# Shift chain moved to the third burst of a step, stack loads issued ahead of it on SyncE, and the last stage's first inputs loaded in three separate steps

## The chip, the cores and the metric

The kernel runs on one core of a Trainium2 chip. The metric is device time in microseconds (us). Five engines work side by side, each through its own instruction list in order: TensorE (PE; its weight loads are shown as PEld), VectorE (DVE), ScalarE (ACT), GpSimd (POOL) and SyncE (SP), which here issues every transfer (DMA). They order one another with semaphores only, written out by hand.

## The reference, cut to what matters

```python
Q = _split_heads(x, H)                 # x: (8, 1024, 256), H = 16 heads of 16
K = _split_heads(x @ Wk + bk, H)
V = _split_heads(x @ Wv + bv, H)       # 64 columns a head
scores = einsum('bhqd,bhkd->bhqk', Q, K) + mask      # causal
attn = softmax(scores, axis=-1)
o = einsum('bhqk,bhkd->bhqd', attn, V)
x = layernorm(x + x + gelu(o) @ Wf + bf)
x = layernorm(x + (silu(x @ wg) * (x @ wu)) @ wd)    # weights: integers / 127
```

## The kernel before, in words

The work has three stages. In stage A the first two of 16 "units" (512 tokens each) are projected to keys and values. Stage B, from about 47 to 1470 us, is attention over 64 pairs of heads; beside it the projection jobs of the other 14 units are done. Stage C is the output product, both layer norms and the feed-forward part, unit by unit.

Stage B is a walk over steps `r`, each of 8 bursts `b`. PE handles pair `r` and pair `r - 2` in one step: for pair `r` it computes 12 score tiles (`score(j)`, here s0 to s11), from which DVE takes row maxima (`top(j)`), and for pair `r - 2` 12 transposed score tiles (`scoreT(t)`, here t0 to t11), which ACT exponentiates, POOL masks and adds up for the denominators, and PE multiplies with V (`weigh`). The 24 tiles go in turn through three PSUM buffers (`ring`), so a tile needs the consumer of an earlier one to be done: scoreT(3) waits for the maximum of s1, scoreT(4) for that of s2, t6 and t7 for those of s4 and s5, and t0 and t1 of the next step for s10 and s11.

A burst holds three tiles: t0, s0, t1 in burst 0; s1, t2, s2 in burst 1; t3, s3, t4 in burst 2; s4, t5, s5 in burst 3; t6, s6, t7 in burst 4, and so on.

The shift chain turns the row maxima of pair `r - 1` into two more rows of that pair's query stack, which are subtracted in the transposed scores. On DVE it is `shift_hi` (a cast of 128x16), `shift_lo` (a subtraction of 128x16) and `shift_turn` (a transpose of 128x32), each needing the one before. SP then stores the result to memory in 4 transfers (`move_shifts`, line 440), waits until they have landed and loads it in 2 (`load_shifts`, line 449). It is needed by scoreT(0) of the next step.

Projection jobs of six matmuls each lie at bursts 6, 7 and 9 counted from a step's start. By `r % 4` (called k0 to k3 here) a step starts 3, 2, 3 or 2 jobs; from step 56 on there are none. In a k0 step `x_part1`, a cast of 128x1024 on DVE, stands behind burst 2.

On SP a step is one list in order, `attend`: the shift transfers, the stacks of pair `r + 1` (`load_stacks`, 4 transfers), V (`load_v`), stores of projected tiles, of the outputs and of the denominators. In step 58 (`PAIRS - 6`) the first inputs of stage C are loaded: `load_g(0)`, `load_g(1)` (2.5 MB each with `xn`) and `load_dn(0)` (2 MB).

DVE's `shift_hi` and `shift_lo`, and POOL's masks and additions, all work from SBUF to SBUF.

Of the kernel before, what the change touches and what calls it, by code (L numbers as in the profile page):

```python
# [93 lines left out]
def build(nc, xT, x, Wk, bk, Wv, bv, Wf, bf, wg, wu, wd, out):  # L94
# [10 lines left out]
    PAIRS = B * H // 2  # L105
# [15 lines left out]
    with ExitStack() as ctx:  # L121
# [239 lines left out]
        def _(sp):  # L361
# [73 lines left out]
            def move_shifts(n):  # L435

                sp.wait_ge(s_shs, n + 1)
                settle(sp, s_passed["sp"])
                for i in range(P // SQ):
                    sp.dma_start(sd[bass.ds(n, 1)].rearrange("o h m (u s q) -> (o h m u) s q", s=P // SQ, q=SQ)[:, i],  # L440
                                  shiftT[SQ * i:SQ * (i + 1), :].bitcast(F32)).then_inc(s_shd, 16)
# [32 lines left out]
            def attend(r, it):  # L474
                n = r + RING * it
                a, k = unit_beside(r, it), r % 4
                if 1 <= r <= PAIRS:
                    move_shifts(n - 1)
                    load_shifts(r - 1, n - 1)
                if r + 1 < PAIRS:  # L480
                    load_stacks(r + 1, it)
                if k == 0 and r >= 4 and unit_beside(r - 4, it) is not None:
                    store_v(unit_beside(r - 4, it), 2)
                    store_v(unit_beside(r - 4, it), 3)
                if r < PAIRS:
                    load_v(r, it)
                if a is not None:
                    if k == 1:
                        store_k(a)
                    if k == 2:  # L490
                        store_v(a, 0)
                        if r // 4 + ALONE + 1 < UNITS:
                            load_x(a + 1)
                    if k == 3:
                        store_v(a, 1)
                if r % 4 == 3 and 7 <= r < 4 * GROUPS + 7:
                    load_den((r - 7) // 4 + it)
                if 3 <= r < PAIRS + 3:
                    store_o(r - 3, n - 3)
                    store_den(r - 3, n - 3)  # L500
                if r % 4 == 1 and 9 <= r < 4 * GROUPS + 9:
                    store_rec((r - 9) // 4 + it)
                if a is not None and k == 0:
                    store_q(a)
                if r == PAIRS - 6:

                    sp.wait_ge(s_job, NJ * UNITS)
                    sp.wait_ge(s_xs, UNITS)
                    sp.wait_ge(s_qst, 16 * 3 * UNITS)
                    sp.wait_ge(s_kst, 16 * 3 * UNITS)  # L510
                    for stored in s_vst:
                        sp.wait_ge(stored, 16 * UNITS)

                    for i in range(2):
                        sp.wait_ge(s_ost[i], 16 * (PAIRS // B // 2))
                    sp.wait_ge(s_rst, 16 * 2)
                    load_g(0, 0)
                    load_g(1, 0)
                    load_dn(0, 0)
                if r == PAIRS + LEAD:  # L520

                    sp.wait_ge(s_st, NS * PAIRS)
                    load_dn(1, 0)
# [497 lines left out]
        def _(dve):  # L1021
# [126 lines left out]
            def attend(r, it):  # L1148
                n = r + RING * it
                a, k = unit_beside(r, it), r % 4  # L1150
                for b in range(NBURST):
                    ended = job_ended(r, it, b)
                    if ended and ended[0] < DC:
                        k_part1(ended[1], ended[0], oo[0][:])
                        k_part2(ended[1], ended[0], oo[0][:])
                    if b == 0 and 1 <= r <= PAIRS:
                        shift_hi(r - 1, n - 1)
                    if b == 5 and LEAD <= r < PAIRS + LEAD:
                        carry_sum(n - LEAD)
                    for what, j in uses(b):  # L1160
                        if what == "s" and r < PAIRS:
                            top(j, r, n)
                        if what == "s" and j == 0 and 1 <= r <= PAIRS:
                            shift_lo(r - 1, n - 1)
                            shift_turn(r - 1, n - 1)
                    if b == 4 and LEAD <= r < PAIRS + LEAD:
                        begin_sum(r - LEAD, n - LEAD)
                    if a is not None and k == 0:
                        if b == 2:
                            x_part1(a)  # L1170
                        if b == 4:
                            x_part2(a)
                    if b == 7 and PAIRS <= r < PAIRS + 2:
                        norm(0, 0, range(4 * (r - PAIRS), 4 * (r - PAIRS + 1)))
                    if b == 7 and r == 0:
                        ffn_weights()
                    if b == 5 and k == 0 and 8 <= r < 4 * GROUPS + 8:
                        reciprocals((r - 8) // 4 + it, r == 8)
# [130 lines left out]
```

## Time and profile before

| what | value |
|---|---|
| median of 3 runs | 1998.43 us (1998.09 to 2004.68) |
| profiled execution, its own time | 1999.08 us |
| span of the profiled execution | 1997.3 us |
| busy: PE, DVE, POOL, ACT | 94%, 77%, 57%, 52% |
| granted TensorE clock, mean over the span | 0.97 of full speed |
| four steps of stage B with jobs, 645.0 to 731.3 us | PE 83.93 us busy of 86.3, granted clock 1.00 |
| interval between the denominator products of two steps, k0 to k1, k1 to k2, k2 to k3, k3 to k0 | 23.5, 20.6, 21.5, 20.7 us |
| the same in undisturbed steps without jobs | 20.4 to 20.5 us |
| a mask on POOL (line 632) | 0.44 us in the mean |

The page gives each engine's busy time and groups of instructions; the timeline gives instructions in order of time, with the engine's idle time before one in brackets and what ended it. PE is busy nearly all the time, so what matters is which short waits it has left, and in which step.

### The profile page before, as it was taken

Reading aid. Unit: us, or ns where it says so; the run is one execution under the profiler, and the core shown is the slowest. Engines: PE = TensorE matmul, PEld = TensorE weight load, DVE = VectorE, ACT = ScalarE, POOL = GpSimd, SP = SyncE. Lnnn points to the kernel's source line nnn. Section 1 sums busy time; section 2 is a strip of 40 time slices with the busy share of each in tenths; the row PEclk is TensorE's granted clock in tenths of the full one; section 3 lists DMA queues with packets and bytes.
Section 4 is the critical chain, followed back from the end, with each engine's and each line's share of the span. In section 5 each row is a group of like instructions: output and inputs, shape, how many; then the busy total and the mean of one; then the engine's idle time right before and its main releaser. Section 6 shows DMA issues by size and latency. Waiting matters only on the chain. (4 is left out here: it accounts for less than half of the span.)

```text
span 1997.3 us, 38522 instructions
## 1 busy us (share of the span) xinstructions
PE 1868.8 (94%) x10304; PEld 968.8 (49%) x10304; DVE 1535.2 (77%) x3597; ACT 1040.6 (52%) x1523; POOL 1139.4 (57%) x1200
## 2 busy tenths in 40 slices
PE   6799999999999999999999999878879999999996
PEld 5344444444444444444444444323337767767673
DVE  3887878888788878878788787767736887878874
ACT  2255555555655555555555555445544555655653
POOL 2177677677677677777777767766831221221212
PEclk9799999999999999999999999889989999999998
DMA  8844545554553545454464464383138666675610
GB/s 270 249 132 143 170 143 162 145 181 139 153 181 110 177 136 173 147 168 160 120 194 147 138 175 126 107 227 86 51 83 212 171 158 181 167 177 173 150 67 21
DMA packets 260962, 303.17 MB, mean 152 GB/s; under 512 B 28048, under 2 KB 177680, under 8 KB 260880
## 3 DMA queue, kind: packets, MB, share of 16 engines
q1 hardware_dynamic: 260880, 302.19, 52.5%
q8 instruction: 38, 0.62, 0.1%
q14 instruction: 44, 0.36, 0.1%
HBM read 174.20 MB, written 127.93 MB: 151 GB/s over the span
## 5 line engine op out<-in xcount | busy, mean ns | idle before, releaser
L936 ACT ACTIVATE weights<-ring 128x1024 f32<-128x1024 f32 (+3 forms) x768 | 601.3, 810 | 357.7 <-PE ring L684 355.2
L654 POOL TENSOR_TENSOR weight_sum<-weight_sum,weights 128x512 f32<-128x512 f32 (+3 forms) x448 | 682.9, 1524 | 9.7
L684 PE MATMUL o_acc<-weights,v_pair 128*64 128x512 f32 (+3 forms) x3072 | 619.4, 510 | 9.5 <-POOL weights L632 8.9
L632 POOL TENSOR_SCALAR_AFFINE_SELECT weights<-weights 128x256 f32<-128x256 f32 x512 | 224.5, 444 | 347.4 <-ACT weights L936 345.7
L1083 DVE TENSOR_REDUCE part_max<-ring 128x2 f32<-128x1024 f32 x256 | 300.2, 1214 | 104.0 <-PE ring L684 103.9
L684 PE MATMUL ring<-q_stack,k_stack 50*128 50x512 f32 (+3 forms) x1536 | 314.1, 414 | 55.2 <-DVE part_max L1083 29.3
L675 POOL TENSOR_TENSOR h_lo<-hidden,h_hi 128x512 f16<-128x512 f32 x96 | 114.5, 1194 | 399.4 <-ACT h_hi L905 399.4
L684 PE MATMUL ring<-k_stack,q_stack 48*128 48x512 f32 (+3 forms) x1536 | 307.3, 403 | 22.2 <-DMA k_stack<-k_rows 12.7
L1091 DVE CUSTOM_DVE_ANT_0 scrap<-ring,causal 128x128 bf16<-128x128 f32 (+3 forms) x512 | 229.3, 485 | 79.8 <-PE ring L684 79.3
L1091 DVE CUSTOM_DVE_ANT_0 scrap<-ring,causal,part_max 128x128 bf16<-128x128 f32 (+3 forms) x512 | 251.3, 547 | 49.6 <-PE ring L684 49.3
L684 PEld LDWEIGHTS o_acc<-weights,v_pair 128*64 128x64 f32 x3072 | 173.5, 137 | 229.9 <-issue 204.4
L684 PEld LDWEIGHTS ring<-q_stack,k_stack 50*128 50x128 f32 x1536 | 145.5, 187 | 276.1 <-DVE part_max L1083 121.6
L684 PEld LDWEIGHTS ring<-k_stack,q_stack 48*128 48x128 f32 x1536 | 147.7, 189 | 206.5 <-ACT weights L936 157.2
L684 PE MATMUL ring<-wf_sb,g 128*128 128x256 f32 x1024 | 233.0, 384 | 8.6 <-DVE y_pre L1201 8.6
L684 PEld LDWEIGHTS ring<-wf_sb,g 128*128 128x128 f32 x1024 | 195.2, 193 | 38.2 <-DVE y_pre L1201 9.0
L905 ACT ACTIVATE v_unit<-o_acc 128x512 f32<-128x512 f32 x112 | 67.0, 599 | 257.0 <-PE o_acc L684 257.0
L1146 DVE TENSOR_TENSOR g<-g,den_wide 128x512 f32<-128x512 f32 x128 | 151.0, 1204 | 1.2 <-DMA g<-o_heads 1.2
L654 POOL TENSOR_TENSOR weight_sum<-weights 128x768 f32<-128x768 f32 x64 | 116.8, 1825 | 0.0
L684 PE MATMUL o_acc<-wv_hi,x_hi 128*128 128x512 f32 x224 | 101.4, 453 | 0.0
L1125 DVE TENSOR_TENSOR weight_sum<-weights 128x1024 f32<-128x1024 f32 x64 | 78.6, 1227 | 16.4 <-PE o_acc L684 16.4
L957 ACT ACTIVATE g<-g,bv_sb 128x512 f32<-128x512 f32 x128 | 80.3, 709 | 18.3 <-DVE g L1146 18.2
L684 PE MATMUL o_acc<-wv_lo,x_hi 128*128 128x512 f32 x224 | 89.2, 398 | 0.0
(105 smaller groups left out, 2153.5 us busy)
## 6 DMA issues: line engine op xcount, KB each, us to landing
v_pairs<-v_unit SPq DMA_DIRECT2D x64, 512.0 KB, 5.6
v_pair<-v_pairs SPq DMA_DIRECT2D x64, 512.0 KB, 5.5
o_heads<-o_pair SPq DMA_DIRECT2D x64, 512.0 KB, 5.3
g<-o_heads SPq DMA_DIRECT2D x16, 2048.0 KB, 8.2
den_wide<-reciprocals SPq DMA_DIRECT2D x32, 1024.0 KB, 13.4
q_stack<-q_rows SPq DMA_DIRECT2D x128, 192.0 KB, 3.5
k_stack<-k_rows SPq DMA_DIRECT2D x128, 192.0 KB, 4.2
q_rows<-x_hi SPq DMA_DIRECT2D x32, 512.0 KB, 5.1
```

The lines of the kernel that those rows point to most:

```text
L632: pool.affine_select(out=diag, in_=diag, compare_op=ALU.is_ge, fill=0.0, base=0, pattern=[[0, 2], [1, P]], channel_multiplier=-1).then_inc ...
L654: pool.tensor_tensor(dst, other, W[t][:, :, :], ALU.add).then_inc(s_add, 1)
L675: pool.tensor_tensor(h_lo[:, f], h32[f % 2][:], h_hi[:, f], ALU.subtract).then_inc(s_hl, 1)
L684: return nc.tensor.matmul(o, l, r, start=start, stop=stop)
L905: return nc.scalar.activation(o, i, ACT.Copy)
L936: nc.scalar.activation(W[t][:, :, :], bank_of("t", t)[:, :, 0:width_of(t)], ACT.Exp).then_inc(s_w, 1)
L957: nc.scalar.activation(g[r % 2][:, c], g[r % 2][:, c], ACT.Gelu, bias=bv_sb[:, c:c + 1]).then_inc(s_gelu, 1)
L1083: v.tensor_reduce(part[r % 2][:, u - 4, :], bank_of("s", j)[:, :, 0:w], AX.X, ALU.max).then_inc(s_max, 1)
L1091: e = v.tensor_tensor_reduce(out=scrap[j % 2][h][:, 0:w], in0=bank_of("s", j)[:, h, 0:w], in1=causal[:, BANK - w:BANK], scale=1.0, scalar= ...
L1125: v.tensor_tensor(acc1[:], W[4][:], W[5][:], ALU.add).then_inc(s_add1, 1)
L1146: v.tensor_tensor(g[r % 2][:, c], g[r % 2][:, c], dn[r % 2][:, c], ALU.mult).then_inc(s_gn, 1)
```

## The change

On DVE the three parts of the shift chain no longer stand in bursts 0 and 1 but together behind burst 2. On SP the two shift steps stand behind the stack loads, the last stores of a unit's V tiles and `load_v`. The load of `g0` stays in step 58; that of the denominators goes to step 60 and that of `g1` to step 62.

```diff
             def attend(r, it):                       # SP
-                if 1 <= r <= PAIRS:
-                    move_shifts(n - 1)
-                    load_shifts(r - 1, n - 1)
                 if r + 1 < PAIRS:
                     load_stacks(r + 1, it)
...
                 if r < PAIRS:
                     load_v(r, it)
+                if 1 <= r <= PAIRS:
+                    move_shifts(n - 1)
+                    load_shifts(r - 1, n - 1)
...
                     load_g(0, 0)
+                if r == PAIRS - 4:
+                    load_dn(0, 0)
+                if r == PAIRS - 2:
                     load_g(1, 0)
-                    load_dn(0, 0)
...
                                                      # DVE
-                    if b == 0 and 1 <= r <= PAIRS:
-                        shift_hi(r - 1, n - 1)
                     if b == 5 and LEAD <= r < PAIRS + LEAD:
                         carry_sum(n - LEAD)
                     for what, j in uses(b):
                         if what == "s" and r < PAIRS:
                             top(j, r, n)
-                        if what == "s" and j == 0 and 1 <= r <= PAIRS:
-                            shift_lo(r - 1, n - 1)
-                            shift_turn(r - 1, n - 1)
...
+                    if b == 2 and 1 <= r <= PAIRS:
+                        shift_hi(r - 1, n - 1)
+                        shift_lo(r - 1, n - 1)
+                        shift_turn(r - 1, n - 1)
```

DVE, before, at the head of a step with k0, between the last row maxima of the step before and those of s4 (the two TENSOR_REDUCE of the first pair are s1 and s2, the second pair s4 and s5; a row "ISA scrap,rowmax" is one head of a maximum):

```order
L1091 ISA scrap,rowmax<-ring,causal 128x128
L1091 ISA rowmax 128x1
L1107 TENSOR_TENSOR shift_parts<-rowmax,shift_parts 128x2x8
L1116 STREAM_TRANSPOSE shiftT<-shift_parts 128x32
L1083 TENSOR_REDUCE part_max<-ring 128x2 x2
L1091 ISA scrap,rowmax<-ring,causal 128x384
L1091 ISA rowmax 128x1
L1091 ISA scrap,rowmax<-ring,causal 128x384
L1091 ISA rowmax 128x1
L1045 CAST x_hi<-xt 128x1024
L1083 TENSOR_REDUCE part_max<-ring 128x2 x2
```

The same place now; the chain has moved from ahead of s1's maximum to behind x_hi's cast, directly ahead of s4's maximum:

```order
L1085 TENSOR_REDUCE part_max<-ring 128x2 x2
L1093 ISA scrap,rowmax<-ring,causal 128x384
L1093 ISA rowmax 128x1
L1093 ISA scrap,rowmax<-ring,causal 128x384
L1093 ISA rowmax 128x1
L1047 CAST x_hi<-xt 128x1024
L1105 CAST shift_parts<-rowmax 128x2x8
L1109 TENSOR_TENSOR shift_parts<-rowmax,shift_parts 128x2x8
L1118 STREAM_TRANSPOSE shiftT<-shift_parts 128x32
L1085 TENSOR_REDUCE part_max<-ring 128x2 x2
```

SP, before, from step 58's last stores into step 59:

```order
L432 DMA o_heads<-o_pair 128x1024
L456 DMA denominators<-den_rows 4x512
L534 DMA g<-o_heads 128x8x512
L536 DMA xn<-in_x 128x4x256
L534 DMA g<-o_heads 128x8x512
L536 DMA xn<-in_x 128x4x256
L547 DMA den_wide<-reciprocals 64x8x512 x2
L440 DMA shifts<-shiftT 32x32 x4
L449 DMA q_stack<-shifts 2x1024 x2
L409 DMA q_stack<-q_rows 48x1x1024 x2
L409 DMA k_stack<-k_rows 48x1x1024 x2
L425 DMA v_pair<-v_pairs 128x8x128
```

The same place now; one of the three big loads is left, and the next step's stacks and V go ahead of the shift transfers:

```order
L432 DMA o_heads<-o_pair 128x1024
L456 DMA denominators<-den_rows 4x512
L536 DMA g<-o_heads 128x8x512
L538 DMA xn<-in_x 128x4x256
L409 DMA q_stack<-q_rows 48x1x1024 x2
L409 DMA k_stack<-k_rows 48x1x1024 x2
L425 DMA v_pair<-v_pairs 128x8x128
L440 DMA shifts<-shiftT 32x32 x4
L449 DMA q_stack<-shifts 2x1024 x2
```

## Rows read from the trace of the kernel before

**Rows 1.** Timeline of SP and PE around step 59 (start, us, engine, line, operation).
```profile
1314.80 2.61 SPq L440 DMA_DIRECT2D shifts<-shiftT  x4
...
1319.55 1.07 PE L684 MATMUL o_acc<-weight_sum,ones 128*32 128x512 f32 x8
...
1333.81 0.79 PE L684 MATMUL ring<-q_stack,k_stack 50*128 50x512 f32 x2 [4.59 <-DMA q_stack<-shifts]
...
1352.03 1.06 PE L684 MATMUL o_acc<-weight_sum,ones 128*32 128x512 f32 x8
```

**Rows 2.** Timeline of DVE, head of a k0 step to burst 3.
```profile
727.94 1.54 DVE L1103 CAST shift_parts<-rowmax 128x16 fp32r<-128x16 f32 x1
...
729.82 1.27 DVE L1107 TENSOR_TENSOR shift_parts<-rowmax,shift_parts 128x16 fp32r<-128x16 f32 x1
731.33 0.21 DVE L1116 STREAM_TRANSPOSE shiftT<-shift_parts 128x32 f32<-128x32 f32 x1 [0.24 <-DVE shift_parts L1107]
...
736.53 2.36 DVE L1083 TENSOR_REDUCE part_max<-ring 128x2 f32<-128x1024 f32 x2 [1.00 <-PE ring L684]
```

**Rows 3.** Timeline of POOL, the same stretch.
```profile
727.61 1.84 POOL L654 TENSOR_TENSOR weight_sum<-weight_sum,weights 128x768 f32<-128x768 f32 x1
...
729.77 1.28 POOL L654 TENSOR_TENSOR weight_sum<-weight_sum,weights 128x512 f32<-128x512 f32 x1
...
734.93 0.86 POOL L632 TENSOR_SCALAR_AFFINE_SELECT weights<-weights 128x256 f32<-128x256 f32 x1
735.77 2.16 POOL L654 TENSOR_TENSOR weight_sum<-weight_sum,weights 128x512 f32<-128x512 f32 x2
```

**Rows 4.** Timeline of PE, the same stretch: scoreT(4), and scoreT(7).
```profile
733.85 0.51 PE L684 MATMUL ring<-q_stack,k_stack 50*128 50x512 f32 x2 [0.45 <-DVE part_max L1083]
...
738.94 0.50 PE L684 MATMUL ring<-q_stack,k_stack 50*128 50x512 f32 x2
```

**Rows 5.** Timeline of PE and DVE in a step without jobs.
```profile
1314.85 0.33 PE L684 MATMUL ring<-q_stack,k_stack 50*128 50x128 f32 x2 [1.70 <-DVE part_max L1083]
...
1315.98 0.50 PE L684 MATMUL ring<-q_stack,k_stack 50*128 50x512 f32 x2 [0.58 <-DVE part_max L1083]
...
1318.61 2.36 DVE L1083 TENSOR_REDUCE part_max<-ring 128x2 f32<-128x1024 f32 x2 [1.74 <-PE ring L684]
```

**Rows 6.** Timeline of POOL, that step: the addition in bursts 2 and 3.
```profile
1315.37 1.82 POOL L654 TENSOR_TENSOR weight_sum<-weights 128x768 f32<-128x768 f32 x1
```

**Rows 7.** Timeline of DVE in stage C: three products back to back.
```profile
1706.82 3.37 DVE L1146 TENSOR_TENSOR g<-g,den_wide 128x512 f32<-128x512 f32 x3
```

**Rows 8.** Timeline of POOL beside them.
```profile
1707.64 1.40 POOL L675 TENSOR_TENSOR h_lo<-hidden,h_hi 128x512 f16<-128x512 f32 x1 [0.16 <-ACT h_hi L905]
```

**Rows 9.** Timeline of DVE: s4's and s5's maxima in a k1 and a k3 step.
```profile
760.03 2.36 DVE L1083 TENSOR_REDUCE part_max<-ring 128x2 f32<-128x1024 f32 x2 [1.74 <-PE ring L684]
...
802.10 2.36 DVE L1083 TENSOR_REDUCE part_max<-ring 128x2 f32<-128x1024 f32 x2 [1.24 <-PE ring L684]
```

**Rows 10.** Timeline of POOL in those two steps.
```profile
758.07 2.17 POOL L654 TENSOR_TENSOR weight_sum<-weight_sum,weights 128x512 f32<-128x512 f32 x2
759.50 0.73 POOL L654 TENSOR_TENSOR weight_sum<-weight_sum,weights 128x256 f32<-128x256 f32 x1
...
800.59 2.16 POOL L654 TENSOR_TENSOR weight_sum<-weight_sum,weights 128x512 f32<-128x512 f32 x2
```

**Rows 11.** Timeline of DVE: two small operations, the second needing the first.
```profile
1717.29 0.17 DVE L1261 SCALAR_TENSOR_TENSOR newton<-mean_var,rstd 128x8 f32<-128x8 f32 x1 [0.61 <-ACT rstd L1015]
1717.50 0.17 DVE L1264 TENSOR_TENSOR newton<-newton,rstd 128x8 f32<-128x8 f32 x1
```

**Rows 12.** Windows: busy time of each engine, granted clock, DMA share, GB/s.
```profile
1270.00:1275.00 5.00, 4.74 (x16) 1.48 (x16) 1.98 (x5) 1.90 (x3) 4.52 (x6) 0.50 0.22 56
```

**Rows 13.** DMA view: transfers, size, median us to landing.
```profile
v_pairs<-v_unit SPq DMA_DIRECT2D x64, 512.0 KB, 5.6
...
shifts<-shiftT SPq DMA_DIRECT2D x256, 4.0 KB, 1.3
```

## Prediction

> **What bounds the kernel now.** I read the page first: PE is busy for 94% of the span, and in four steps with jobs for 83.9 of 86.3 us, so there all waits that a change could take away sum to 2.4 us. Then I read the timeline of PE step by step, taking the denominator products as marks, to see which short waits are left, and the timelines of DVE and POOL beside them, to see what makes them.
>
> Three things stand out. First, one step is far too long: between the marks at 1319.55 and 1352.03 lie 32.48 us, where a step without jobs takes 20.45 [rows 1]. SP issued the shift transfers of that step behind seven MB of loads for stage C; they went out at 1314.80 and PE still waited for the shift rows at 1333.81 (4.59 us), and again 4.59 us for the next stack behind them, with the clock at its lower level afterwards.
>
> Second, the shift chain costs DVE far more than its work. The cast of 128x16 took 1.54 us and ended at 729.48, when POOL's addition ended (727.61 + 1.84 = 729.45); the subtraction took 1.27 and ended at 731.09, when POOL's next addition ended (729.77 + 1.28 = 731.05) [rows 2, 3]. Each began just after POOL's. The smallest such operations take 0.17 us. So DVE and POOL exclude one another in these operations, for the whole of an instruction. The Trainium skill says the same (SBUF — State Buffer, "Who interferes with whom": a cast in a 2-port mode or an operation with two SBUF inputs blocks or is blocked by GpSimd for a whole instruction), and the trace agrees.
>
> Third, who waits: behind the chain stand the maxima of s1 and s2, and scoreT(3) and scoreT(4) need them. In a k0 step PE waited 0.45 us at scoreT(4) [rows 4]; the k1 and k2 steps have the same row with 0.39 and 0.46, k3 none. In a step without jobs PE waited 1.70 + 0.58 us [rows 5].
>
> **The big loads.** In the new order step 58 ends with 2.5 MB, step 60 with 2 MB, step 62 with 2.5 MB. The old seven MB went out from 1301.9 on and the shift rows behind them were there only at 1333.8 [rows 1], some 30 us, so a third of them takes about 10 us; it is issued some 15 us into a step of 20 and is over before the next step's shift transfers, which are also later now. I take the whole excess as gone: 32.48 - 20.45 = **-12.0 us**. If one part is still felt, this is less (a rival below).
>
> **The chain's old place.** Without it the maxima of s1 and s2 come as early as PE allows. With jobs, scoreT(4) comes 0.45 (k0), 0.39 (k1), 0.46 (k2) and 0 us (k3) earlier. Without jobs s1 is ready at 1312.3, its maximum takes half of 2.36, s2's the other half, so scoreT(4) can start at about 1314.71 and not 1315.98 [rows 5]: 1.27 us earlier.
>
> **The chain's new place.** It stands ahead of s4's maximum, where DVE idled for 1.00 to 1.74 us [rows 2, 5, 9]. But this gap is not free time. The two maxima of s4 and s5 end at 736.53 + 2.36 = 738.89, and scoreT(7), which needs s5's, starts at 738.94 [rows 4]; in each kind of step I found these 0.05 us. Every microsecond by which s4's maximum starts later than 0.54 us behind the start of its matmul is one that PE waits at scoreT(6) and (7). So I have to place the chain against POOL. Three prices: the cast ends 0.03 us behind the POOL operation it waits for; the subtraction asks 0.04 later (a dependent small operation started at 1717.50 behind one that ended at 1717.46 [rows 11]); the transpose comes 0.24 later and takes 0.21 [rows 2]. And a rule: three DVE products back to back took 3.37 us from 1706.82, and POOL's operation from 1707.64 to 1709.04 ran between the first two [rows 7, 8]. So whoever already waits goes next, and the engine that has just finished does not keep the right.
>
> - k0: x_hi's cast ends at 736.53 - 1.00 = 735.53. POOL's mask (734.93, 0.86 long, so itself held up) goes next and ends at 735.79, the chain's cast at 735.82, and the addition from 735.77, which was already waiting, holds the subtraction until 735.77 + 1.28 = 737.05 [rows 3]. The transpose ends at 737.53; s4's maximum starts at 737.47 instead of 736.53: **+0.94 us**.
> - k1: DVE is free at 760.03 - 1.74 = 758.29, POOL's addition has just begun at 758.07 and ends at 759.35, the second one starts only at 759.50 because it depends on the first [rows 9, 10]. The cast ends at 759.38, the subtraction asks at 759.42, 0.08 us ahead of the second addition, and gets in; the transpose ends at 760.04: s4's maximum starts at 759.98, **-0.05**.
> - k2: the cast waits for the end of an addition at 779.2, the subtraction for a mask, until 779.6; the transpose ends at 780.05, ahead of s4's maximum at 780.22. The gain stands whole: **-0.46**.
> - k3: DVE is free at 802.10 - 1.24 = 800.86, POOL's addition began at 800.59 and ends at 801.87. As in k1 the subtraction gets in ahead of the second one; the transpose ends at 802.57, s4's maximum starts at 802.52: **+0.42**.
> - without jobs: DVE is free at about 1315.62, the addition of 1.82 us that began at 1315.37 holds the cast until 1317.2 [rows 6], a mask the subtraction until 1317.6, and s4's maximum starts at 1317.93 where it started at 1318.61 [rows 5]: **-0.68**.
>
> Four steps with jobs: 0.94 - 0.05 - 0.46 + 0.42 = +0.85 us, a small loss. There are 13 such groups (steps 4 to 55): **+11.1 us**. Seven steps without jobs (57 to 63): 7 x -0.68 = **-4.8 us**. The steps ahead of 4 and behind 63 have nothing on POOL beside the chain: 0.
>
> **The clock.** In stage B without jobs the granted clock fell to 0.50, the lower of the two levels (1.2 GHz), for some microseconds in three steps, each time behind PE's waits at scoreT(3) and (4) [rows 12]; these steps took 23.07, 21.91 and 22.03 us instead of 20.45, together 5.7 us more. The waits there shrink from 2.28 to about 1.0 us, with 0.6 put in at scoreT(6). Four steps with the full waits did not lose the clock, so this is no switch; between 0 and 5.7 I take half: **-2.8 us**.
>
> **SP.** The shift transfers now go out about 6 us later in a step. The stack loads need the previous step's last scoreT and go out at once; load_v and the V stores stand ahead of the shift transfers. In k0 the last V store waits for ACT's copy of the last job (about 5.6 us into the step), load_v for that store's landing (5.6 us [rows 13]), so the shift transfers go out some 12 us into the step, queue behind 512 KB (5.6 at most), then the loads: about 19 us, in a step of 23.5. In the other steps they land about 15 us into 20.6. The stores behind them (keys, V, outputs) come up to 6 us later, and their readers stand in later steps. Cost 0, hidden by the rest of the step, 4.5 us in the tightest case.
>
> **The sum.** -12.0 + 11.1 - 4.8 - 2.8 = -8.5 us against the execution's own 1999.08, which lies 0.65 above the median: 1990.6; against the median 1989.9. I say **1990 us**. The step's own range is 1982 to 1998.
>
> **Rivals.**
> 1. *The second addition wins.* In k1 and k3 the subtraction beats POOL's second addition by 0.08 us only. Losing it costs 0.73 less the 0.1 us or so of overlap: +0.6 in each, +1.2 in a group, 13 groups: +15.6, time 2006. For it: the margin is smaller than what I know of each price, and the skill's page cited above says only that whoever starts first holds the port. Against it: POOL's pause between the two is in both steps. 15%.
> 2. *The chain is hidden.* DVE gets in sooner than I placed it, in k0 above all, or the loss there is swallowed by a later wait. At the far end nothing is lost at s4: 13 x -1.3 = -17, 7 x -1.27 = -9, -12 and the whole clock term -5.7: 1955. Getting only k0 free (-1.4 a group, -18) gives 1972. For it: the idle time is there; against it: the ends of POOL's and DVE's operations coincide within 0.04 us. 17%, most of it near 1972.
> 3. *Slower: the shift rows come too late.* In k0 steps the chain of store, load_v, shift store and shift load has 4.5 us of room by my count. If each landing takes 2.5 us longer than in the median, scoreT(0) of the k1 step waits; with 3 us in 13 steps this is +39, about 2029. It decides from some 5 us later than computed. For it: the landings are medians and 1.3 us [rows 13] was taken where nothing else was in flight. The Trainium skill gives a DMA a fixed cost of about 2 us (DMA: Bandwidth & Descriptors, "Anatomy of one DMA"), longer than this row; by it two landings would come 1.4 us later, still inside the room. 11%.
> 4. *The loads are still felt.* One of the three parts delays a stack or shift rows as much as all together did: -12 becomes 0, time 2002. 7%.
>
> The forecast has 50%. Faster by over 0.5% (10 us, about what a measurement of this kernel can tell from no change) means below 1988.4: rival 2 and two fifths of the forecast, 0.37. Slower means above 2008.4: rival 3 and a little of rival 1: 0.13. The rest, 0.50, is the same. The range of 1970 to 2012 leaves out the far ends of rivals 2 and 3.
>
> **What the changed profile would show.** The step with the big load back at 20 to 22 us and no wait for shift rows or stacks. No wait at scoreT(3) in job steps, and none or less at scoreT(4). The cast at burst 3 at 0.3 to 1.6 us, ending with a POOL addition; the subtraction long (about 1.2 us) in k0 and short in k1 and k3. New waits of PE for DVE at scoreT(6) or (7), about 0.9 us in k0, 0.4 in k3. The groups of four at about 87.1 us instead of 86.3. I am wrong if these groups get shorter, if the subtraction is long in k1 and k3 too, or if PE waits for "q_stack<-shifts" at the head of steps.

## The result, and the profile after

The kernel after takes 2019.08 us in the median (2015.39 to 2020.07), the kernel before 1998.26 in the runs beside it: ratio 1.0096, 95% interval 1.0069 to 1.0124. It is slower by about 1%, where I forecast 1990. The profiled execution took 2019.51 us, 20.4 more than that of before.

The page's head, with busy time and share of each engine:

```profile
span 2017.8 us, 38472 instructions
...
PE 1863.2 (92%) x10304; PEld 967.2 (48%) x10304; DVE 1547.3 (77%) x3597; ACT 1043.9 (52%) x1523; POOL 1126.2 (56%) x1200
```

PE's share fell from 94 to 92%. DVE is busy 12 us longer than before (1535.2), although it does the same operations: more of its time is time in which it stood blocked. Windows of the kernel after, first four steps with jobs, then three without (us, busy time and count of PE, PEld, DVE, ACT, POOL, granted clock, DMA share, GB/s):

```profile
647.85:736.61 88.76, 84.07 (x478) 37.34 (x476) 71.10 (x172) 47.80 (x69) 62.42 (x68) 0.98 0.52 150
...
1308.76:1329.67 20.91, 17.11 (x107) 6.65 (x105) 17.95 (x41) 11.21 (x16) 15.42 (x18) 1.00 0.33 92
1329.67:1352.38 22.71, 18.65 (x106) 7.12 (x104) 18.23 (x42) 11.18 (x16) 16.04 (x18) 0.92 0.71 199
1352.38:1372.99 20.61, 17.11 (x106) 6.65 (x105) 17.39 (x45) 11.22 (x16) 14.91 (x18) 1.00 0.35 94
```

The group of four took 86.3 us and takes 88.76. PE's busy time in it is nearly the same (83.93 and 84.07), so PE waits 2.3 us more. The interval behind step 59's mark, which took 32.48 us [rows 1], is the window of 20.61 now: the big load's stall is gone. The window of 22.71 is the one before it, 20.45 in before; it has the longest of the new waits (below) and a granted clock of 0.92. What PE waits for stands in its timeline (denominator products of a k0, k1, k2, k3 and k0 step are the rows with `weight_sum,ones`; the first two waits are those of the k2 step, then those of k0; the last rows are from a step without jobs):

```profile
668.32 1.07 PE L686 MATMUL o_acc<-weight_sum,ones 128*32 128x512 f32 x8
...
693.83 1.07 PE L686 MATMUL o_acc<-weight_sum,ones 128*32 128x512 f32 x8
...
714.06 1.06 PE L686 MATMUL o_acc<-weight_sum,ones 128*32 128x512 f32 x8
715.91 0.50 PE L686 MATMUL ring<-q_stack,k_stack 50*128 50x512 f32 x2 [0.78 <-DVE part_max L1085]
...
717.04 0.50 PE L686 MATMUL ring<-q_stack,k_stack 50*128 50x512 f32 x2 [0.51 <-DVE part_max L1085]
...
736.61 1.06 PE L686 MATMUL o_acc<-weight_sum,ones 128*32 128x512 f32 x8
...
757.09 1.07 PE L686 MATMUL o_acc<-weight_sum,ones 128*32 128x512 f32 x8
759.81 0.50 PE L686 MATMUL ring<-q_stack,k_stack 50*128 50x512 f32 x2 [1.66 <-DVE part_max L1085]
...
760.94 0.65 PE L686 MATMUL ring<-q_stack,k_stack 50*128 50x512 f32 x2 [0.51 <-DVE part_max L1085]
...
1324.97 0.33 PE L686 MATMUL ring<-q_stack,k_stack 50*128 50x128 f32 x2 [0.59 <-DVE part_max L1085]
...
1326.10 0.50 PE L686 MATMUL ring<-q_stack,k_stack 50*128 50x512 f32 x2 [0.58 <-DVE part_max L1085]
...
1332.35 0.50 PE L686 MATMUL ring<-q_stack,k_stack 50*128 50x512 f32 x2 [1.62 <-DVE part_max L1085]
...
1333.48 0.50 PE L686 MATMUL ring<-q_stack,k_stack 50*128 50x512 f32 x2 [0.51 <-DVE part_max L1085]
```

The marks stand behind scoreT(4) and ahead of scoreT(6). The intervals between them are 25.51 (k0 to k1), 20.23, 22.55 and 20.48 us; in before they were 23.5, 20.6, 21.5 and 20.7. The wait at scoreT(4) [rows 4] is gone in these steps, and waits at scoreT(6) and scoreT(7) have come: 2.17 us in k0, 1.29 in k2.

Part of the loss in k0 is clock. In the 13 groups of before the granted clock was 1.00 from end to end. In the kernel after it fell to 0.50, the lower of the two levels, for some microseconds in 12 of the 13 intervals k0 to k1, each time right behind these two waits of PE. The first window is an interval that kept the clock, the second one that lost it, the third lies inside the second:

```profile
225.75:250.58 24.83, 21.70 (x125) 9.77 (x123) 21.93 (x52) 11.52 (x17) 17.03 (x18) 1.00 0.55 161
668.32:693.83 25.51, 22.96 (x125) 10.30 (x123) 21.88 (x52) 11.59 (x17) 16.48 (x18) 0.93 0.51 156
673.00:675.00 2.00, 2.00 (x8) 0.48 (x6) 2.00 (x2) 1.02 (x1) 0.00 (x0) 0.50 0.03 8
```

Eleven such intervals took 25.39 to 25.65 us, and the first, where the lower level stayed longer, 26.92. Against the 24.83 of the one without it that is some 9 us in the 13 groups. The k2 steps, with waits of 0.78 and 0.51 us, kept the clock.

DVE at the same places shows the reason for the waits:

```profile
711.81 2.25 DVE L1105 CAST shift_parts<-rowmax 128x16 fp32r<-128x16 f32 x1
714.10 0.18 DVE L1109 TENSOR_TENSOR shift_parts<-rowmax,shift_parts 128x16 fp32r<-128x16 f32 x1
714.52 0.21 DVE L1118 STREAM_TRANSPOSE shiftT<-shift_parts 128x32 f32<-128x32 f32 x1 [0.25 <-DVE shift_parts L1109]
714.65 2.33 DVE L1085 TENSOR_REDUCE part_max<-ring 128x2 f32<-128x1024 f32 x2
...
754.62 2.73 DVE L1047 CAST x_hi<-xt 128x1024 fp32r<-128x1024 f32 x1
757.27 0.70 DVE L1105 CAST shift_parts<-rowmax 128x16 fp32r<-128x16 f32 x1
758.01 0.17 DVE L1109 TENSOR_TENSOR shift_parts<-rowmax,shift_parts 128x16 fp32r<-128x16 f32 x1
...
758.56 2.33 DVE L1085 TENSOR_REDUCE part_max<-ring 128x2 f32<-128x1024 f32 x2
...
1326.91 3.68 DVE L1105 CAST shift_parts<-rowmax 128x16 fp32r<-128x16 f32 x1
```

And POOL beside them:

```profile
710.57 1.85 POOL L656 TENSOR_TENSOR weight_sum<-weights 128x768 f32<-128x768 f32 x1
712.34 0.44 POOL L634 TENSOR_SCALAR_AFFINE_SELECT weights<-weights 128x256 f32<-128x256 f32 x1
712.72 2.19 POOL L656 TENSOR_TENSOR weight_sum<-weight_sum,weights 128x512 f32<-128x512 f32 x2
...
753.35 1.84 POOL L656 TENSOR_TENSOR weight_sum<-weights 128x768 f32<-128x768 f32 x1
755.12 0.44 POOL L634 TENSOR_SCALAR_AFFINE_SELECT weights<-weights 128x256 f32<-128x256 f32 x1
755.49 2.45 POOL L656 TENSOR_TENSOR weight_sum<-weight_sum,weights 128x512 f32<-128x512 f32 x2
...
1327.11 1.84 POOL L656 TENSOR_TENSOR weight_sum<-weights 128x768 f32<-128x768 f32 x1
1328.89 0.42 POOL L634 TENSOR_SCALAR_AFFINE_SELECT weights<-weights 128x256 f32<-128x256 f32 x1
1329.27 2.17 POOL L656 TENSOR_TENSOR weight_sum<-weight_sum,weights 128x512 f32<-128x512 f32 x2
```

In the k2 step the cast stood ready at 711.81, while the addition of 710.57 ran. It did not get in when that ended (712.42), nor when the mask behind it ended (712.78). It ended at 714.06, at the end of the next addition, where POOL has its one pause (the two additions of the row of 712.72 depend on each other and lie 0.15 us apart). In the k0 step x_hi's cast, 0.87 us long before, waited in the same way and took 2.73. In the step without jobs the shift cast took 3.68 us for work of 0.17. That is the longest of the seven such steps; two of the others got in at the first end (0.24 and 0.23 us).

The whole difference, by marks of the two traces, where the loads and the chain are still mixed: up to the mark of step 4 +1.8 us, the 13 groups (steps 5 to 56) +32.6, steps 57 to 63 -15.3, steps 64 to 66 +1.7, the rest -0.4.

### The profile page after: what moved, and what is told of

The parts are those of the page before. It is cut to its first block and busy times, and to the rows that moved or that the text cites. A ratio compares the mean times of both kernels' runs of the same rounds, so it can differ in the third digit from the quotient of the medians.

```text
span 2017.8 us, 38472 instructions
## 1 busy us (share of the span) xinstructions
PE 1863.2 (92%) x10304; PEld 967.2 (48%) x10304; DVE 1547.3 (77%) x3597; ACT 1043.9 (52%) x1523; POOL 1126.2 (56%) x1200
## 5 line engine op out<-in xcount | busy, mean ns | idle before, releaser
L686 PE MATMUL o_acc<-weights,v_pair 128*64 128x512 f32 (+3 forms) x3072 | 629.3, 517 | 14.9 <-POOL weights L634 10.1
L634 POOL TENSOR_SCALAR_AFFINE_SELECT weights<-weights 128x256 f32<-128x256 f32 x512 | 211.1, 418 | 392.0 <-ACT weights L938 378.4
L686 PE MATMUL ring<-q_stack,k_stack 50*128 50x512 f32 (+3 forms) x1536 | 308.7, 405 | 79.3 <-DVE part_max L1085 68.6
L686 PE MATMUL ring<-k_stack,q_stack 48*128 48x512 f32 (+3 forms) x1536 | 302.1, 396 | 18.3 <-DMA k_stack<-k_rows 9.0
```

The source lines that it names most:

```text
L634: pool.affine_select(out=diag, in_=diag, compare_op=ALU.is_ge, fill=0.0, base=0, pattern=[[0, 2], [1, P]], channel_multiplier=-1).then_inc ...
L686: return nc.tensor.matmul(o, l, r, start=start, stop=stop)
```

## The experiments

The kernels of the experiments were timed in five rounds each; a ratio is to the kernel before on the same chip. For each, the length of two stretches of its profiled execution: the 13 groups with jobs, and steps 57 to 63.

| kernel | median us | ratio, 95% interval | 13 groups | 57 to 63 |
|---|---|---|---|---|
| before | 1998.3 | | 1119.6 | 160.8 |
| after | 2019.1 | 1.0069 to 1.0124 | 1152.2 | 145.5 |
| chain only | 2033.1 | 1.0150 to 1.0192 | 1150.8 | 160.0 |
| SP order only | 1999.1 | 0.9986 to 1.0014 | 1119.1 | 161.2 |
| three loads only | 1987.1 | 0.9924 to 0.9961 | 1119.3 | 148.7 |
| after, two-input first part | 2016.7 | 1.0068 to 1.0108 | 1151.3 | 144.4 |
| after, pause ahead of mask 3 | 1985.2 | 0.9909 to 0.9950 | 1122.8 | 141.2 |
| after, two short additions | 1961.0 | 0.9785 to 0.9830 | 1099.2 | 140.7 |
| after, chain behind fourth burst | 2012.1 | 1.0037 to 1.0082 | 1148.0 | 141.4 |
| three loads only, same pause | 1986.8 | 0.9919 to 0.9960 | 1119.5 | 148.7 |
| after, pause ahead of mask 2 | 1988.2 | 0.9923 to 0.9967 | 1124.2 | 142.9 |
| chain behind fourth burst, pause | 1990.9 | 0.9944 to 0.9973 | 1127.0 | 143.6 |
| pause, k0's chain behind fourth burst | 1979.4 | 0.9879 to 0.9923 | 1115.8 | 141.6 |
| pause, x_hi behind fourth burst | 1969.9 | 0.9837 to 0.9884 | 1107.1 | 142.7 |

### The three parts of the change alone

**Chain only**: the kernel before with the DVE part of the change.

```diff
-                    if b == 0 and 1 <= r <= PAIRS:
-                        shift_hi(r - 1, n - 1)
...
-                        if what == "s" and j == 0 and 1 <= r <= PAIRS:
-                            shift_lo(r - 1, n - 1)
-                            shift_turn(r - 1, n - 1)
...
+                    if b == 2 and 1 <= r <= PAIRS:
+                        shift_hi(r - 1, n - 1)
+                        shift_lo(r - 1, n - 1)
+                        shift_turn(r - 1, n - 1)
```

> The kernel before with one part of the change: the three shift operations on DVE behind burst 2; SP's order and the big loads as before. Theory P (the cast waits for POOL through several operations in a row, ahead of the maximum of s4, and PE then waits at scoreT(6) and (7)): all of the loss is here. From the changed kernel's steps: +34 us up to step 56, some -3 in the steps without jobs, +2 behind them, and the 12 us of the big load stay: about 2030 us. Rival S (the later shift transfers on SP, or the loads ahead of them, make the loss): no loss here, 1998 or a few us less, since scoreT(3) and (4) no longer wait.

**SP order only**: the two shift steps behind `load_v`.

```diff
-                if 1 <= r <= PAIRS:
-                    move_shifts(n - 1)
-                    load_shifts(r - 1, n - 1)
...
                     load_v(r, it)
+                if 1 <= r <= PAIRS:
+                    move_shifts(n - 1)
+                    load_shifts(r - 1, n - 1)
```

> The kernel before with SP's new order alone: stack loads, V stores and load_v ahead of the shift transfers, DVE and the big loads as before. Theory P: no difference but in the step with the big load, 1990 to 1999 us. Rival S: slower by 20 us or more, with waits of PE for shift rows or stacks.

**Three loads only**:

```diff
                     load_g(0, 0)
+                if r == PAIRS - 4:
+                    load_dn(0, 0)
+                if r == PAIRS - 2:
                     load_g(1, 0)
-                    load_dn(0, 0)
```

> The kernel before with the last stage's first inputs loaded in steps 58, 60 and 62 and nothing else changed. By the prediction's term the long step shrinks from 32.5 to 20.5 us and the whole by 12: 1986 us. If each part is felt alone, between 1990 and 1998.

Measured: +34.3, +0.4 and -11.7 us to the before of the same chip (1998.77). They add to +23.0, where all together gave +20.8. So the SP order is neutral, the loads gave what they should, and the whole loss is the chain's place on DVE. With the chain alone the interval with the big load's stall takes 38.2 us instead of 32.48, which is part of the 34.3.

### What kind of operation waits

The chain's first part as an operation with two SBUF inputs (the maximum of the row maxima with themselves, the same values) instead of a cast:

```diff
-                v.tensor_copy(shift_parts[:, :, 0], rowmax[r % 2][:]).then_inc(s_shp, 1)
+                v.tensor_tensor(shift_parts[:, :, 0], rowmax[r % 2][:], rowmax[r % 2][:],
+                                ALU.max).then_inc(s_shp, 1)
```

> The changed kernel with the cast of shift_hi written as a maximum of the row maxima with themselves, a TENSOR_TENSOR with two SBUF inputs that gives the same values. In both traces all 65 subtractions that met POOL got in at the end of the very next POOL operation, while the cast at burst 3 did so in 3 of about 70 cases where POOL's operations followed without a pause. Theory P, with the kind of operation deciding: the first operation now lasts at most 1.8 us (until POOL's next end), 0.3 in k2 steps where it was 2.25, up to 1.8 where it was 3.7; gain 1.5 x 13 in k2 steps and about 1 x 7 without jobs: 1990 to 1997 us. If only the place among POOL's operations decides and not the kind: 2019 as the changed kernel.

Measured: 2016.74, as the kernel after. DVE's timeline, the k2 step:

```profile
709.43 2.20 DVE L1105 TENSOR_TENSOR shift_parts<-rowmax 128x16 fp32r<-128x16 f32 x1
```

It waits 2.20 us where the cast waited 2.25. That it could pass where a cast can't is refuted: the kind of operation does not matter, only that it comes first at this place.

### A pause in POOL's run

If DVE gets in only where POOL pauses, a pause one addition earlier must let it in. POOL's fourth mask waits for the end of the addition just ahead of it, which is a wait of some 0.17 us and orders nothing new:

```diff
             def mask(t, rt, n):
                 pool.wait_ge(s_w, NS * n + t + 1)
+                if t == 3:
+                    pool.wait_ge(s_add, NA * n + 1)
                 settle(pool, s_passed["pool"])
```

> The changed kernel with one more wait on POOL: the mask of t3 waits for the first addition of the pair, which stands directly ahead of it, so that POOL pauses there some 0.15 us as it does between its second and third additions. At that pause DVE got in every time. Theory P (DVE gets in only where POOL pauses, once POOL has run for long without one): the first shift operation in k2 steps ends 0.03 us behind the first addition (0.3 us instead of 2.25) and the interval k2 to k3 falls from 22.5 to about 21; x_hi's cast in k0 steps takes 0.8 to 1 instead of 2.7 and the interval k0 to k1 falls from 25.5 to 24.4 or less. 13 x 2.6 and 7 x 1: about 1980 us. Rival K (POOL's total work in this stretch delays DVE, the pause changes nothing): 2019 to 2022.

> Control to the pause: the kernel with the three separate loads and the chain in its old place, 1987.1 us, with the same added wait on POOL. The pause by itself should cost nothing (POOL is idle 5 us a step) and may let x_hi's cast in earlier in the few steps where it was held up: 1984 to 1989. If the wait itself gives or takes time, it shows here.

Measured: 1985.18 us, 34 less than the kernel after; the same pause with the chain in its old place (beside the three loads) gives 1986.75, where the loads alone gave 1987.12. So the pause costs and gives nothing by itself, and it takes nearly the whole of the chain's +34 away. DVE in a k2 step of the kernel with the pause:

```profile
698.16 0.64 DVE L1107 CAST shift_parts<-rowmax 128x16 fp32r<-128x16 f32 x1
698.84 0.17 DVE L1111 TENSOR_TENSOR shift_parts<-rowmax,shift_parts 128x16 fp32r<-128x16 f32 x1
```

and POOL:

```profile
696.95 1.82 POOL L658 TENSOR_TENSOR weight_sum<-weights 128x768 f32<-128x768 f32 x1
698.94 0.41 POOL L636 TENSOR_SCALAR_AFFINE_SELECT weights<-weights 128x256 f32<-128x256 f32 x1 [0.17 <-POOL weight_sum L658]
```

The cast ends 0.03 us behind the addition (698.77), as my prediction had it for the kernel after. The shorter waits also cost less clock: it fell in 5 of the 13 groups instead of 12. Two k0 to k1 intervals of this kernel have the same waits (0.77 and 0.5 us) and take 24.57 us with the lower level in them and 23.86 without.

**Short additions**: POOL's second and third additions cover only the last 8 of their 512 columns, so the denominators lack the rest of these sums.

```diff
+                if t in (2, 3):
+                    pool.tensor_tensor(dst[:, :, w - 8:w], other[:, :, w - 8:w],
+                                       W[t][:, :, w - 8:w], ALU.add).then_inc(s_add, 1)
+                else:
+                    pool.tensor_tensor(dst, other, W[t][:, :, :], ALU.add).then_inc(s_add, 1)
```

> The changed kernel with most of POOL's second and third additions of each pair left out: they add the last 8 columns of each head alone, so the denominators are incomplete and only the time is read. Theory P: the first shift operation can at most wait for the first addition and a mask and then meets a pause, so the chain no longer delays s4's maximum by more than 0.5 us: 2.8 us less in a group of four steps, 1.5 in a step without jobs, 1970 to 1985. If PE's waits at scoreT(6) and (7) have another cause than POOL's additions: 2010 to 2019.

Measured: 1961.01, below what I expected. The groups take 84.6 us; the waits at scoreT(6) and (7) are gone but for 0.4 us in k0, and the clock never fell in them. It agrees with POOL's operations being all that stands in the chain's way, but it also takes work from POOL that other operations of DVE waited for, so it gives a bound and not a share.

### Is it the pause, or how long POOL has run?

The place of the cast and the length of POOL's run ahead of it were mixed up till then. This kernel pauses one place earlier, ahead of the third mask; the end of the 768-wide addition and the mask behind it are back to back again, only soon after a pause:

```diff
+                if t == 2:
+                    pool.wait_ge(s_sel, NM * n + masked(1))
```

> As the kernel after, but POOL's pause stands one place earlier: ahead of the third mask (mask 2) instead of ahead of the fourth, so the end of the first addition (128x768) and mask 3 behind it are back to back again, only that POOL has by then run three operations (about 2.7 us) since its last pause instead of 13 or more. Theory 1 (the length of POOL's unbroken run decides whether the waiting DVE operation gets in between two back-to-back POOL operations): the cast gets in at the end of the first addition, as with the pause at that place, and the time is near 1985. Theory 2 (the place decides: the boundary between that addition and the mask never lets DVE in, or only a real pause does): the casts in k2 and in the steps without jobs wait until the pause behind the second addition, as in the kernel after, and the time stays near 2017. A third result would be casts that get in at the earlier pause only in k3 and k1: 2005 to 2015. I expect theory 1 with 60%.

Measured: 1988.16. DVE, a k2 step:

```profile
698.28 0.81 DVE L1107 CAST shift_parts<-rowmax 128x16 fp32r<-128x16 f32 x1
699.12 0.32 DVE L1111 TENSOR_TENSOR shift_parts<-rowmax,shift_parts 128x16 fp32r<-128x16 f32 x1
```

POOL beside it:

```profile
696.87 0.41 POOL L636 TENSOR_SCALAR_AFFINE_SELECT weights<-weights 128x256 f32<-128x256 f32 x1 [0.16 <-POOL weights L636]
697.24 1.82 POOL L658 TENSOR_TENSOR weight_sum<-weights 128x768 f32<-128x768 f32 x1
699.01 0.41 POOL L636 TENSOR_SCALAR_AFFINE_SELECT weights<-weights 128x256 f32<-128x256 f32 x1
699.38 1.28 POOL L658 TENSOR_TENSOR weight_sum<-weight_sum,weights 128x512 f32<-128x512 f32 x1
```

The addition ends at 699.06, the cast at 699.09 and the subtraction at 699.44, at the end of the mask. At exactly this end of the addition, of the casts that stood waiting (19 shift casts and 13 of x_hi), none of 32 got in in the kernel after, and 32 of 32 do here. The first theory holds in this comparison: a real pause at the place itself is not needed, one two operations earlier is enough. In the kernel after two subtractions did get in at this end, both 0.03 us behind a cast that had itself just got in.

### Where else to put the chain

**Chain behind the fourth burst**, no pause:

```diff
-                    if b == 2 and 1 <= r <= PAIRS:
+                    if b == 3 and 1 <= r <= PAIRS:
                         shift_hi(r - 1, n - 1)
```

> The changed kernel with the shift chain one burst later, behind the maxima of s4 and s5, where POOL's third addition ends and POOL is then idle for about 6 us. Theory P: the three operations take 0.17 + 0.17 + 0.24 + 0.21 us, nothing waits at scoreT(6) and (7); s6's maximum comes some 0.4 us later, which may cost 0 to 0.3 a step at scoreT(9). Against before the waits at scoreT(4) are gone (1.3 us in four steps with jobs, 1.3 in each without) and so are the 12 us of the loads: 1955 to 1975 us. If the chain costs wherever it stands behind burst 2 (or its later transfers come too late): 1998 or more.

Measured: 2012.07, a miss. The chain itself runs free there, but the 13 groups are as long as after. DVE, a k0 step:

```profile
662.26 2.49 DVE L1047 CAST x_hi<-xt 128x1024 fp32r<-128x1024 f32 x1
...
666.93 0.16 DVE L1105 CAST shift_parts<-rowmax 128x16 fp32r<-128x16 f32 x1
```

PE, the same step:

```profile
667.07 0.50 PE L686 MATMUL ring<-q_stack,k_stack 50*128 50x512 f32 x2 [0.52 <-DVE part_max L1085]
...
672.80 0.44 PE L686 MATMUL ring<-q_stack,k_stack 50*128 50x384 f32 x2 [1.48 <-DVE rowmax L1093]
```

x_hi's cast, which was not moved, is blocked all the same. It took 0.87 to 1.23 us in the groups of before, 2.6 to 2.9 in the three kernels with the chain behind the third burst, full additions and no pause (but for one of 1.14), and about 2.5 here. The clock adds to it: it fell in 11 of the 13 groups, each time behind the row-maximum wait of 1.3 to 1.5 us, and these intervals k0 to k1 took 25.6 to 26.0 us where the two others took 24.3 and 24.5. That is some 17 of the 28.4 us by which the groups are longer than before. The chain at the head of a step had broken POOL's run: in before its cast ended at 729.48 and its subtraction at 731.09 [rows 2, 3], and x_hi's cast got in a few operations later. I had not asked what the chain did for others while it stood there.

**The same, with the pause ahead of mask 3**:

> As the kernel with the chain behind the fourth burst (2012), plus POOL's pause ahead of mask 3. If that kernel's loss was x_hi's cast, which took 2.5 us in each k0 step across four POOL operations and made all behind it late, the pause shortens the cast to about 1.3 us or less, the wait at the next ring tile of that step (1.72 us at a score whose row maximum is late, and 0.52 at scoreT(7)) shrinks by about 1.2 us, and 13 steps give 15 us: 1996. If the chain in front of s6's maximum is what costs, nothing changes in these steps: 2010 to 2013.

Measured: 1990.93, so 21 us of that kernel's time came with the long run of POOL, the clock that it cost among them (it falls in 6 groups here, in 11 there). x_hi takes 0.9 us in it. A row-maximum wait of 1.25 us in k0 stays: behind the fourth burst come x_lo's subtraction and the two sums, and the chain makes the maxima behind them late.

**Pause, and only k0's chain behind the fourth burst** (`b == (3 if k == 0 else 2)`):

```diff
-                    if b == 2 and 1 <= r <= PAIRS:
+                    if b == (3 if k == 0 else 2) and 1 <= r <= PAIRS:
                         shift_hi(r - 1, n - 1)
```

> As the kernel with the pause (1985), but in k0 steps alone the chain stands behind the fourth burst, so that it does not follow x_hi's cast ahead of s4's maximum. The part_max wait of 1.3 us at scoreT(6) and (7) in that step goes down to about 0.3, the row maxima behind the chain come some 0.7 us later. Theory A (two small DVE operations and x_hi together are too much for the gap): 0.6 to 1.0 us a group less, 1972 to 1978. Theory B (what is saved at s4 is given back at s6 and s7, as in the kernel with all chains behind the fourth burst): 1985 to 1992.

**Pause, chain in its new place, x_hi's cast behind the fourth burst**:

```diff
                     if a is not None and k == 0:
-                        if b == 2:
+                        if b == 3:
                             x_part1(a)
```

> As the kernel with the pause (1985), but x_hi's cast stands behind the fourth burst instead of the third, and the chain stays behind the third. The chain in k0 then looks like that in k2: a cast of about 0.6 us and no long subtraction. x_hi's 0.69 us then stand ahead of s6's maximum, with x_lo's subtraction of 1.22 behind it. Theory A: as for the kernel with the chain moved in k0: 1972 to 1980. Theory B: the maxima of s6 and s7 are late and the row-maximum wait of 0.2 to 0.6 us becomes 1.5 us or more: 1985 to 1995.

Measured: 1979.42 and 1969.92, one a little above and one a little below what I expected of theory A. Neither saving was given back: x_hi's cast takes its own 0.68 us in the last kernel, the k0 to k1 interval is 22.98 us (23.5 in before, 25.51 in after) and a row-maximum wait of 0.74 us is left in it. Its clock stayed at 1.00 in all 13 groups. Its window of four steps:

```profile
627.11:712.44 85.33, 83.05 (x478) 36.89 (x476) 67.59 (x172) 47.46 (x69) 63.19 (x68) 1.00 0.53 156
```

This version beats both kernels: 0.9861 of before, 29 us, of which 12 are the loads.

## Why the prediction was wrong

**What bounds the kernel, and who excludes whom**: right. PE's short waits for DVE, and the clock lost behind them, made the loss, and the chain's first operation ends 0.03 us behind a POOL operation in every case I looked at. Only which one was wrong.

**The big loads**, -12.0: right; alone -11.7.

**SP's new order**, 0: right (ratio 1.0000). PE never waits for a shift row in the kernel after, so rival 3 falls, though it had the right side and nearly the right time, which was luck. (The section that it names for the 2 us of a DMA gives them for transfers issued by GpSimd; here SP issues them, and rows 13 have 1.3.) The others fall with the rows: in k1 and k3 the subtraction is short (rival 1), the chain is not hidden (rival 2), and no shift row or stack waits for the loads (rival 4).

**The chain's old place**: right in job steps. In steps without jobs the waits at scoreT(3) and (4) shrank from 2.28 [rows 5] to 0.59 + 0.58, near the 1.0 I took.

**The chain's new place**, +11.1 for the 13 groups: here it failed. They cost +32.6. The sentence that fails is "whoever already waits goes next, and the engine that has just finished does not keep the right". I had it from one row, where POOL waited and DVE had run [rows 7, 8], and used it the other way round.

The table goes by the intervals between the marks. The gain at scoreT(4) falls ahead of a step's mark and the waits at scoreT(6) and (7) behind it, so my shift for k0 becomes 0.94 + 0.45 - 0.39 = 1.00 for the interval k0 to k1 (its own gain is already spent, that of k1 falls into it), and the others likewise; the sum stays 0.85. Measured are the means of the 13 groups, with the sum 2.5.

| interval | predicted | measured | what the trace shows |
|---|---|---|---|
| k0 to k1 | +1.00 | +2.1 | x_hi's cast 2.73 us instead of 0.87, then a shift cast of 0.70; some 0.7 of it is clock |
| k1 to k2 | -0.12 | -0.4 | DVE asks during the addition that ends at POOL's pause |
| k2 to k3 | 0.00 | +1.1 | shift cast 2.25 us, over the ends of two POOL operations |
| k3 to k0 | -0.03 | -0.3 | as k1: cast 1.12, subtraction 0.18 |

In k1 and k3 the cast happened to wait for the addition ahead of the pause, and the placing was right, even a little dark. In k2 and k0 it asked one addition earlier, and the rule mattered. Besides, for k0 I took x_hi's cast as it was and did not ask whether it would be as short without the chain ahead of it.

**The clock in the groups**, put at nothing without a word: a second step that failed, and a smaller one. I gave the clock a term in the steps without jobs alone. It fell in 12 of the 13 groups behind the new waits and cost some 9 of the 32.6 us.

**Steps without jobs and the clock**, -4.8 - 2.8 = -7.6: the kernel after has -3.2 to the kernel with the three loads only (148.7 to 145.5 us). The cast took up to 3.68 us instead of 1.6, and up to 1.62 + 0.51 us of waits came at scoreT(6) and (7) where I put in 0.6. The granted clock was 0.92 in three of the seven steps, again behind waits, so that term gave little. With the pause the same stretch gives -7.5 (148.7 to 141.2).

**The check by the pause**: with it the shift cast of k2 behaves as my rule had it. Steps 57 to 63 come out as predicted and the sum at 1985 against 1990. Its 13 groups cost +3.2 against +11.1, and by its own intervals some 4 us of clock (5 times 0.7) are in the 3.2, so there my working was too dark. That this one rule carried the error, waits and clock together, is shown by it, and by the kernel with the earlier pause (1988).

**What stays open**: why POOL's run matters. That DVE gets in soon after a pause and not late in a run is shown for this one end of an addition. Whether operations or microseconds count, and where the bound lies, was not tried, and the length of the run is not the whole of it. In the traces of before and after, all shift operations that asked with POOL at most 8 operations past its last pause got in at the first end (9.3 us past it at most; I leave out a few that asked within 0.04 us of an end), and all operations that were passed over asked during the 12th or later (8.9 us or more past the pause). But of five shift casts that asked during the 13th operation, in steps without jobs of the kernel after, two got in at its end and three did not, and the rows do not show why. In before 10 of 13 casts of x_hi asked during the 14th and got in at its end. That the chain's operations, which had got in 3.6 us earlier, reset the run there as a pause does is argued from these casts and from the two subtractions named above, not tried by itself. Nor was it tried what makes the clock fall behind one wait and not behind an equal one.

## What to carry to other kernels

A DVE operation that excludes POOL and is excluded by it is not always priced by the end of the POOL operation beside it. Look how long POOL has run without a break; late in a long run, price it to POOL's next pause as the worse case. If DVE's place is fixed, a pause on POOL (a wait on its own last operation, 0.15 to 0.17 us here, free where POOL has slack) is a cheap door. Before moving a blocked operation away, ask whom it let in while it stood there. And where PE is nearly always busy, look at the granted clock behind each new wait: the wait may cost more than its length.

## What the runs showed of the hardware

- A blocked DVE operation waited through up to four back-to-back POOL operations: 3.68 us for a cast of 128x16 that takes 0.17 free. The Trainium skill (SBUF — State Buffer, "Who interferes with whom") says that whoever issues first holds the shared port pair for the whole instruction. The trace agrees for one instruction; that the same engine may keep the pair over several in a row is what the runs add.
- A cast and an operation with two SBUF inputs were held up alike (2.25 and 2.20 us). The same page names both kinds as ones that contend, and the run agrees.
- A pause of 0.16 or 0.17 us in POOL's run, at the place or two operations ahead, cut the loss of the 13 groups from 32.6 to 3.2 and 4.6 us.
- Behind PE's waits of 1.66 and 0.51 us the granted clock fell from 1.00 to 0.50 for some microseconds: the interval then took about 25.5 us instead of 24.83. With waits of 0.7 to 1.0 and 0.5 us (kernel with the pause) it fell in 5 of 13 groups and cost 0.7 us each time.
